# A third layer on one core: the order of near product, turning, image product and rest

## The reference, cut to what matters

```python
h = jnp.maximum(_layernorm(x, axis=-1), 0.0)
w = adj / jnp.maximum(adj.sum(axis=1, keepdims=True), 1e-08)
log_ij = _logmap(h[:, None, :], h[None, :, :], c)       # for every pair of nodes i, j
agg = jnp.einsum('ij,ijc->ic', w, log_ij)
transformed = agg @ weight + bias
x = x + _expmap(jnp.zeros_like(transformed), transformed, c)
```

## Time and profile before

| | |
|---|---|
| times of three runs | 1118.75, 1117.7, 1115.41 us, median 1117.7 |
| the profiled execution | 1117.01 us |
| its span, first to last instruction | 1115.3 us |
| mean granted TensorE clock | 0.979 |
| PE, PEld busy | 93%, 40% |
| DVE, ACT, POOL busy | 78%, 69%, 25% |
| third layer, first score product to last near gather | about 572 to 1004 us |

### The profile page before, as it was taken

The page is one execution under the profiler, slowest core; times in us unless marked ns, Lnnn a source line. Parts: engine busy times, 40 slices in busy tenths (PEclk is TensorE's granted clock), DMA queues, the critical chain, the costliest instruction groups (busy, mean ns, idle before and its releaser), DMA issues.

```text
span 1115.3 us, 14769 instructions
## 1 busy us (share of the span) xinstructions
PE 1035.8 (93%) x5372; PEld 450.9 (40%) x5372; DVE 867.6 (78%) x1003; ACT 765.9 (69%) x803; POOL 276.3 (25%) x145
## 2 busy tenths in 40 slices
PE   4899999999659999999998999999999998989898
PEld 1233333336643333333333443444544454436454
DVE  6999989996476666688668987877779887887781
ACT  2455554553456656686678889988888889897682
POOL 3179300000010000004005464444343433430010
PEclk9999999998879999999999999999999999999999
DMA  7999999991008888787763445555645545445451
GB/s 258 408 381 360 355 349 322 362 358 62 1 1 292 278 292 278 261 274 272 254 212 126 157 132 155 185 174 172 184 151 189 159 143 170 132 143 197 135 169 38
DMA packets 96324, 238.30 MB, mean 214 GB/s; under 512 B 16384, under 2 KB 45056, under 8 KB 79872
## 3 DMA queue, kind: packets, MB, share of 16 engines
q1 hardware_dynamic: 87040, 220.62, 59.0%
q10 hardware_dynamic: 9216, 16.78, 3.9%
HBM read 219.55 MB, written 17.83 MB: 213 GB/s over the span
## 4 chain that ended last, share of the span: by engine, by line
PE 70%; DVE 15%; ACT 8%; issue 4%; DMA 1%; POOL 1%; SPq 1%; DVEq 0%; ACTq 0%; POOLq 0%
PE PS L537 48%; PE PS L683 5%; PE PS L684 5%; PE PS L780 4%; PE PS L811 4%; DVE work L1870 2%; DVE TB L1421 1%; DVE ring L1876 1%; DVE work L1858 1%; ACT work L1158 1%; ACT work L1150 1%; DMA ring<-in_adj_t 1%; DVE work L1864 1%; ACT work L1081 1%; ACT work L1161 1%
## 5 line engine op out<-in xcount | busy, mean ns | idle before, releaser
L1547 DVE TENSOR_TENSOR work<-work,ring 128x1024 f32<-128x1024 f32 x128 | 151.1, 1222 | 78.8 <-ACT work L1081 78.7
L1018 ACT ACTIVATE work<-PS 128x1024 uint8<-128x1024 f32 x128 | 124.1, 1021 | 120.5 <-PE PS L537 120.5
L1081 ACT ACTIVATE work<-PS,att_sc 128x1024 f32<-128x1024 f32 x128 | 147.6, 1202 | 80.2 <-PE PS L684 72.6
L515 POOL TENSOR_TENSOR ring<-work,ring 128x1024 f32<-128x1024 f32 x57 | 135.2, 2373 | 237.2 <-DVE work L1870 237.2
L537 PE MATMUL PS<-ring,work 128*65 128x256 f32 (+1 forms) x600 | 190.0, 464 | 3.7 <-DVE work L1897 3.7
L537 PE MATMUL PS<-work 128*64 128x512 f32 (+2 forms) x800 | 153.6, 526 | 1.1 <-ACT work L1144 1.0
L1864 DVE SCALAR_TENSOR_TENSOR work<-PS,work 128x1024 f32<-128x1024 f32 x72 | 88.0, 1222 | 56.6 <-PE PS L537 48.4
L537 PEld LDWEIGHTS PS<-ring,work 128*65 128x65 f32 x600 | 80.5, 138 | 90.6 <-issue 65.5
L683 PE MATMUL PS<-work 128*128 128x512 f16 x256 | 98.6, 385 | 4.2 <-DVE work L1370 2.5
L1150 ACT ACTIVATE work<-work 128x1024 f32<-128x1024 f32 x72 | 75.9, 1054 | 35.2 <-DVE work L1858 35.2
L684 PE MATMUL PS<-work 128*128 128x512 f16 x256 | 98.0, 383 | 0.0
(11 more groups left out here) (248 smaller groups left out, 1485.2 us busy)
## 6 DMA issues: line engine op xcount, KB each, us to landing
ring<-in_adj_t SPq DMA_DIRECT2D x96, 1024.0 KB, 5.3
ring<-in_adj_t SPq DMA_DIRECT2D x104, 512.0 KB, 4.1
work<-in_adj_t SPq DMA_DIRECT2D x32, 1024.0 KB, 7.8
codes<-work ACTq DMA_DIRECT2D x64, 256.0 KB, 6.9
ring<-codes SPq DMA_DIRECT2D x64, 256.0 KB, 3.8
H<-in_adj_t SPq DMA_DIRECT2D x24, 512.0 KB, 4.1
X<-in_x SPq DMA_DIRECT2D x2, 512.0 KB, 5.3
out_x<-X SPq DMA_DIRECT2D x1, 512.0 KB, 4.2
```

What stands on the lines that cost most here:

```text
L515: nc.gpsimd.tensor_tensor(near(n), sums(n), near(n), ALU.mult).then_inc(sem("near_ready"), 1)
L1018: nc.scalar.activation(made[:, k, u * UNIT:(u + 1) * UNIT], PS[:, (4 + 2 * u) * BANK:(6 + 2 * u) * BANK], ACT.Relu).then_inc(sem("codes_ma ...
L1081: nc.scalar.activation(att[:, u, :], PS[:, (4 + 2 * u) * BANK:(6 + 2 * u) * BANK], ACT.Sigmoid, bias=att_sc[:, 2:3], scale=att_sc[:, 1:2]) ...
L1547: V.tensor_tensor(prob[:, m % 4, :], att[:, u, :], ring[:, s % RING, u * UNIT:(u + 1) * UNIT], ALU.mult)\
```

## The change

In PE's loop the near gather of unit n-2 goes ahead of the turning of unit n-1, and the far gather stays behind it. In DVE's loop the rest of unit n+1 goes ahead of the image product of unit n-1. Nothing else differs: the same instructions with the same waits.

```diff
@@ PE, step n
                 if n == 1:
                     pe.wait_ge(sem("sums_out1"), 2)
                     to_nodes(ident[:, :], 2 * UNIT, 0).then_inc(sem("support_ready"), 1)
+                if n >= 2:
+                    gather2_near(n - 2)
                 if 1 <= n <= NU and mirrored(n - 1):
                     mirror2(n - 1)
-                if n >= 2:
-                    gather2_near(n - 2)
-                    if mirrored(n - 2):
-                        gather2_far(n - 2)
+                if n >= 2 and mirrored(n - 2):
+                    gather2_far(n - 2)
                 if n in FLIPS:
                     second_half2(FLIPS.index(n))
                 second_aux2(n)
@@ DVE, step n
                 if n >= 3 and closes(n - 3) and n - 3 not in EARLY:
                     near2_out(n - 3)
                 sum2(n)
+                if n + 1 < NU:
+                    rest2(n + 1)
                 if n >= 1 and mirrored(n - 1):
                     far2(n - 1)
-                if n + 1 < NU:
-                    rest2(n + 1)
                 second_half2(n)
                 last_passage2(n)
```

## The result

The changed kernel took 1155.1 us (median of 4 runs, 1154.71 to 1156.71) against 1117.1 (4 runs): ratio 1.0346, interval 1.033 to 1.0362. Slower, as forecast, but by 38 us where 24.9 were forecast: 1155.1 lies above the range. The profiled execution took 1155.4 us.

A forecast was written before the change was run, and what follows sets the result against it. The prediction took PE, with 70% of the chain, to bound the kernel. Order costs in the third layer, 7.0+1.5+1.4+11.9+3.1 = +24.9 us, on 1117.0 gave 1141.9 us; range 1125 to 1148.

The forecast's parts named there:

- PE and DVE, undisturbed: Third-layer steps without disturbance: period stays 5.85 us, turning starts 1.77 after the side products, DVE's image product waits for it.
- The rest beside POOL: DVE's rest, started during POOL's near product, is held until POOL's end, with 0.48 us from there to the next operation.
- Rival 1: Third layer: the rest runs freely beside POOL; +11.7 us, 1129 us in all; chance 0.25.
- A: Units 3 to 11, where DVE also finishes layer two and has next to no slack: +7.0 us.
- B: Segment openings at steps 16 and 22: near gather waits for the near write-out, turning stands behind it; +1.5 and +1.4 us.
- C: PE's turned tangents and features wait for later DVE extras (steps 41, 51, 57); with openings 30 to 54, +11.9 us.
- D: Tail of the third layer: openings at 62 and 68, and ACT getting rest 66 late; +3.1 us.
- The clock: TensorE at half clock after PE's gaps: one stretch costs some 1.7 us, more gaps perhaps +5; not in the sum.
- rival 4: Third layer: stalls halve the clock repeatedly and ACT falls behind after late rests; 1151 us; chance 0.10.

The follow-up runs named there:

- 2: Kernel before with only DVE's edit (rest ahead of the image product), PE's order as before: 1138.1 us, ratio 1.0199.
- 10: Kernel before with only DVE's edit, and POOL's near product cut to the first 512 of 1024 elements: 1121.5 us, ratio 1.0036.
- 4: Changed kernel with POOL's near product cut to the first 512 of 1024 elements: 1138.8 us, ratio 1.0194.
- 9: Kernel before with POOL's near product cut to the first 512 of 1024 elements, as a control: 1114.9 us, ratio 0.998.
- 5: Changed kernel with idle transposes filling PE's gaps at seven openings and ahead of turned tangents and features (212 more matmuls): 1148.7 us, ratio 1.0276.
- 12: Kernel before with the near gather ahead of the turning only in steps 15, 16, 21, 22, write-outs of 13 and 19 early: 1117.5 us, ratio 0.9998.
- the halves: Kernel before with only one engine's edit each: PE's alone 1146.5 us, ratio 1.0258; DVE's alone 1138.1 us, ratio 1.0199.

## Why the prediction was wrong in size and right in kind

By its own steps:

- **PE and DVE, undisturbed: right.** The period held (5.85 forecast, 5.84 measured), turning stands 1.77 behind the side products, and DVE waits ahead of L1876.
- **The rest beside POOL: right**, and the choice that mattered most. Held until 0.55 us after POOL's end (0.48 forecast, to the operation that follows), mean 1079 ns (forecast 0.8 to 1.7), worth 14.0 us by 2 and 10, and 13.7 by 4 and 9. Rival 1, the free rest, fell: it gave 1129.
- **A: slightly low.** Pair product 11 came at 654.94 (near 653.5 forecast), 8.3 us late where 7.0 were forecast by then; with the gap of step 10 filled (5) it was 6.9. So the excess is half clock behind the wait of 4.05 us before near gather 8, an opening for which the forecast added 1.1 us.
- **B: the waits at openings right, the price short.** In the changed kernel 3.7 and 5.2 us came between pair products 11, 17 and 24, where 1.5 and 1.4 were forecast. At 22 it is for 2.9 us the half clock worked out above. The other part lies before step 16: PE waited 3.0 us for POOL's side factors (L501), 0.9 before, as their building took 9.2 us instead of 8.4, and then ran 6.8 us at half clock. The forecast had these steps as hanging on pair product 11 alone. What that stretch cost is open: in 5 it was not there, another of 3.4 us came in step 16, and pair products 11 to 17 took the same 3.7 us more.
- **C: about right.** +14.75 us from pair product 24 to 58 (13.1 with fillers) against 11.9. The openings in steps 30 and 38 gave 0.58 and 0.57 for 0.67, the one in step 46 3.0 for 2.3. The three waits for turned tangents and features were 2.28, 2.81 and 2.27 for 2.4, 2.95 and 2.4.
- **D: low.** +8.2 for 3.1; 4.1 with fillers. The waits of 4.6 and 4.9 us before near gathers 60 and 66 are each followed by half clock (3.4 and 6.8 us).
- **The clock: the step that failed.** The prediction saw the row at 593, priced a stretch at 1.7 us, wrote that "more gaps might bring that two or three times (+5)", and left even that out of the sum; only rival 4 held it, with a chance of 0.10. The same text listed nine openings and three turned operands as new waits of PE, and the one stretch before stood behind gaps of 1.5 and 2.6 us at 589 to 593; it gave no reason why the new ones should be free. There were eight stretches, six of them at these twelve waits, with 16.4 us more of PE busy, about 9.2 of it on the path. Without those the layer grew by 30.9 us (5) for 24.9 forecast. That the clock is the largest miss and not the only one shows in the time of 5 too: 1148.7, still 0.7 above the range.
- **Rival 4** gave 1151 with a clock paid three times and ACT late. The clock was its mechanism and paid more; ACT was not late behind the rests (its waits for L1858 fell from 35.2 us to 13.1). 1155.1 lies above this rival too.

The 6.0 us between 30.9 and 24.9 are spread: 2.2 before step 17 (the side factors, and in 5 the stretch in step 16), 1.7 up to 24, 1.2 in C, 1.0 in D, less 0.1 in A. Those after step 17 were not taken apart further.

## What to carry to other kernels

On an engine that works its queue in order, moving work ahead of a wait pays only where the moved work is itself ready; ask for each step what *it* waits for, and what its producer does just before. When a change opens gaps on PE, count them, and put into the range a price of half clock for each, read from one such stretch already in the trace. It is a risk and not a fixed sum: the changed kernel had 16.4 us more of PE busy beside 23.7 us more of waiting, DVE's half 3.8 beside 17.3. A DVE operation like this rest (f32 `tensor_scalar`, SBUF to SBUF) that is moved into the time of a POOL product waits for its end.

## What the runs showed of the hardware

- **A held DVE operation.** In the changed kernel all 49 rests that began more than 0.1 us before the end of a near product of POOL ended 0.55 or 0.56 us after it (739.55 and 740.10, 636.03 and 636.59), nearly as if they had only begun then, and took up to 1.94 us; 20 that met no near product took 0.69 in the mean. POOL's own product was not lengthened (2.36 beside it, 2.37 in the earlier trace rows). DVE's sum beside POOL, with one operand in PSUM, kept its 1.22, 64 times. By the rule of the Trainium skill (SBUF — State Buffer, "🔬 SBUF: two separate sides"), GpSimd and a DVE operation that runs in a 2-port mode or has two SBUF inputs share a pair of ports, and the first of the two takes it for its whole instruction; the trace agrees: the rest, which takes 0.69 us for as many elements as the sum does in 1.22, waits, and the sum, whose other input is in PSUM, does not. That the rest runs in such a mode no row shows.
- **A gap of PE can cost twice.** At waits of 2.2 to 4.9 us, and in 12 of 1.5, the granted clock fell to 1.2 GHz for 3.4 or 6.8 us. The same four gathers took 3.65 us there and 1.88 with the gap filled by idle transposes. The waits of 2.28 and 2.27 at 841 and 953 brought no such stretch, nor did the one of 2.96 in 5 that had brought 6.8 us in the changed kernel, nor the 1.48 in before that brought 3.4 in 12. So not every gap pays, and which do stays open here. The Trainium skill (TensorE: Matmul & The Clock Gate, "HAM oscillation — how this bites in real kernels") prices work that restarts cold after each wait at half of the time spent throttled. Here that is half of 34.0 us more, 17; the trace agrees, with 16.4 more of PE busy.
- **Costs that share a wait do not add.** 29.0 and 20.6 us for the halves made 38. That the two edits lengthen some of the same waits fits this, and was not tried wait by wait.
